# The second hypergraph layer's node table starts as a copy of x, and its rows are scaled before they are added

## The reference

```python
norm_n2e, norm_e2n = De_inv[edge_idx], Dn_inv[node_idx]   # 1/count of the hyperedge, of the node
def _layer(x, ..., W_n2e, W_e2n):
    h = x @ W_n2e
    e = relu(segment_sum(norm_n2e[:, None] * h[node_idx], edge_idx))
    h2 = e @ W_e2n
    return segment_sum(norm_e2n[:, None] * h2[edge_idx], node_idx)
x1 = relu(_layer(x, W0_n2e, W0_e2n))
x2 = _layer(x1, W1_n2e, W1_e2n)
x  = layernorm(x + x2)
```

## Time and profile before

| | |
|---|---|
| median of 3 runs | 6743.85 us (6737.83 to 6748.29) |
| profiled execution, first to last instruction | 6891.4 us |
| POOL busy | 4010.9 us (58%) |
| DVE busy | 4783.1 us (69%) |
| PE busy | 4257.5 us (62%) |
| ACT busy | 3305.7 us (48%) |
| DMA | 1634.06 MB, mean 237 GB/s |
| HBM | read 816.50 MB, written 813.62 MB |

### The profile page before, as it was taken

How to read it: one execution, slowest core, us unless ns; L and a number is a source line. 1 busy time by engine, 2 the same in 40 slices (tenths; PEclk the granted TensorE clock), 3 DMA queues, 4 the chain that set the end, 5 groups by cost and what they waited for, 6 DMA issues and landing times. The chain is left out here.

```text
span 6891.4 us, 79060 instructions
## 1 busy us (share of the span) xinstructions
PE 4257.5 (62%) x18989; PEld 3141.2 (46%) x18989; DVE 4783.1 (69%) x15487; ACT 3305.7 (48%) x7376; POOL 4010.9 (58%) x3167
## 2 busy tenths in 40 slices
PE   2568883038885788499866677988885677600000
PEld 1247773037774666377612223547774566500000
DVE  6635544645454877599599996866665999587666
ACT  0023331013332555288656665758885788633333
POOL 4757776757775788767155426611113666277776
PEclk9779996569998999799978778989998899855555
DMA  7845445864544999799688988989996677477665
GB/s 278 287 121 79 76 75 147 335 197 75 79 76 89 328 350 351 219 326 342 200 293 304 312 273 318 379 290 328 331 336 222 231 258 247 175 261 242 236 227 193
DMA packets 646111, 1634.06 MB, mean 237 GB/s; under 512 B 128454, under 2 KB 283878, under 8 KB 630290
## 3 DMA queue, kind: packets, MB, share of 16 engines
q1 hardware_dynamic: 459954, 1234.83, 51.9%
q0 software_dynamic: 185696, 394.18, 21.4%
HBM read 816.50 MB, written 813.62 MB: 237 GB/s over the span
## 5 line engine op out<-in xcount | busy, mean ns | idle before, releaser
L822 POOL DMA_INDIRECT NS<-e_tot,e_idx x392 | 648.6, 1655 | 298.1 <-ACT e_tot L1080 222.4
L2304 ACT ACTIVATE l_z<-l_a,l_nb,l_rs 128x256 f32<-128x256 f32 x1176 | 612.7, 605 | 411.3 <-DMA out_dram<-l_z,k_ids 248.1
L1691 POOL DMA_INDIRECT l_eg<-HBT,k_nsrc x392 | 461.8, 1178 | 391.2 <-DVEq L1916 151.3
L956 DVE TENSOR_SCALAR e_eq<-e_pk,z_skey 128x128 f32<-128x128 f32 x588 | 204.2, 348 | 637.1 <-DMA NS<-e_tot,e_idx 608.1
L2181 POOL DMA_INDIRECT out_dram<-l_z,k_ids x392 | 432.0, 1102 | 150.9 <-issue 115.1
L1734 PE MATMUL l_pb<-l_jx,k_ones 128*128 128x128 f32 x26 | 4.3, 304 | 788.3 <-DVE l_jx L1971 788.3
L1080 ACT ACTIVATE e_tot<-e_pa 128x520 f32<-128x520 f32 x196 | 118.6, 605 | 759.7 <-DMA NS<-e_tot,e_idx 748.6
L2226 PE MATMUL l_pm<-k_w_L3b,l_zt 128*128 128x258 f32 x1568 | 404.5, 417 | 126.8 <-ACT l_o L2274 121.8
L2475 DVE BATCH_NORM_STATS2 l_bs<-l_a 128x6 f32<-128x256 f32 x1176 | 467.2, 420 | 10.5 <-issue 3.5
L1223 POOL DMA_INDIRECT XH<-n_o,z_home x392 | 398.0, 1015 | 118.1 <-issue 113.1
L2342 ACT ACTIVATE l_a<-l_a,l_eshare 128x64 f32<-128x64 f32 (+1 forms) x1372 | 382.0, 371 | 124.4 <-DVE l_eshare L1953 67.6
(11 more groups left out here) (409 smaller groups left out, 13538.8 us busy)
## 6 DMA issues: line engine op xcount, KB each, us to landing
NS<-z_zero SPq DMA_DIRECT2D x200, 520.0 KB
HBT<-l_o SPq DMA_DIRECT2D x196, 528.0 KB
l_a<-HBT SPq DMA_DIRECT2D x196, 528.0 KB
GSUMS<-l_erun SPq DMA_DIRECT2D x72, 1056.0 KB
l_a<-XH SPq DMA_DIRECT2D x98, 528.0 KB
HA<-n_o SPq DMA_DIRECT2D x98, 528.0 KB
l_a<-HA SPq DMA_DIRECT2D x98, 528.0 KB
n_r<-NS SPq DMA_DIRECT2D x98, 520.0 KB
```

What stands on the lines that cost most here:

```text
L822: pool.indirect_dma_start(out=nodes, out_offset=bass.IndirectOffsetOnAxis(ap=idx[q % DEEP][:, k:k + 1], axis=0), in_=tot[q % 2][:, k, :], ...
L1691: pool.indirect_dma_start(out=self.g[b % self.ng][:, k, :], out_offset=None, in_=self.table, in_offset=bass.IndirectOffsetOnAxis(ap=self.i ...
L2304: last = act.activation(z[:, j, 0:D], a[:, j, 0:D], ACT.Identity, bias=self.nb[b][:, col:col + 1], scale=self.rs[b][:, col:col + 1])
```

## The change

In e1 the clears of NS1 are replaced by copies of x's blocks into NS1, from DRAM to DRAM, at the same place in SP's list: 97 of 512 rows by 256 floats and one of 336 rows. Two small clears of the rows that x does not have (256 dummy rows and 128 rows from N on) come ahead of them. NS1's rows are 256 floats (1024 bytes) and no longer carry a count. The reciprocal counts that DVE makes in the gather half are kept for all 49 tiles (inv is [128, 49, 4]), and ACT's copy of the two sums becomes two activations, one per column, each scaled by that column's inv. PE's sums have 256 columns in e1 in place of 260. The node stage loads NS1 alone (8 slots), its count, reciprocal and add steps go, and statistics are taken from what was loaded. e0 stays as it was: zeros, counts, one copy.

```diff
+def copy_rows(eng, table, x, n, sem):
+    if n == TAILN:
+        eng.dma_start(table[TAIL0:N, :].rearrange("(p j) w -> p (j w)", j=J), x[TAIL0:N, :].rearrange("(p j) w -> p (j w)", j=J)).then_inc(sem, 16)
+    else:
+        eng.dma_start(table[n * BLK:(n + 1) * BLK, :].rearrange("(p j) w -> p (j w)", j=J),
+                      x[n * BLK:(n + 1) * BLK, :].rearrange("(p j) w -> p (j w)", j=J)).then_inc(sem, 16)
+def clear_spare_rows(eng, table, zero, sem):
+    spare = NPAD - 2 * P
+    eng.dma_start(table[spare:NPAD, :].rearrange("(p j) w -> p j w", j=2), zero[:, 0:2, 0:D]).then_inc(sem, 16)
+    eng.dma_start(table[N:N + P, :], zero[:, 0, 0:D]).then_inc(sem, 16)
...
-        inv = [s.sb(f"inv{b}", [P, J]) for b in range(2)]
+        inv = s.sb("inv", [P, TR, J]) if scaled else None
...
-                            pool.wait_ge(clear, 16 * CLEARS)
+                            pool.wait_ge(clear, 16 * filled)
...
-                        pe.matmul(pa[:, 0, 0:SW], e[:, 0, :], mt[:, 0, :], start=True, stop=False)
+                        pe.matmul(pa[:, 0, 0:ow], e[:, 0, :], mt[:, 0, 0:ow], start=True, stop=False)
...
-                        act.activation(tot[q % 2][:], pa[:, :, 0:SW], ACT.Copy).then_inc(s_cp, 1)
+                        if scaled:
+                            for k in range(2):
+                                c = column(q) + k
+                                last = act.activation(tot[q % 2][:, k, :], pa[:, k, 0:ow], ACT.Copy, scale=inv[:, c // J, c % J:c % J + 1])
+                        else:
+                            last = act.activation(tot[q % 2][:], pa[:, :, 0:ow], ACT.Copy)
+                        last.then_inc(s_cp, 1)
...
+                        if x is not None and tick == 0:
+                            clear_spare_rows(sp, nodes_of, S["zero"], sem)
                         for n in range(n0 + (n1 - n0) * tick // TR, n0 + (n1 - n0) * (tick + 1) // TR):
-                            clear_rows(sp, nodes_of, S["zero"], n, sem)
+                            if x is None:
+                                clear_rows(sp, nodes_of, S["zero"], n, sem)
+                            else:
+                                copy_rows(sp, nodes_of, x, n, sem)
...
-    RA, RR, RO = 7, 4, 7
+    RA, RO = 8, 8
...
-                            sp.dma_start(a[t % RA][:], A["x"][t * BLK:(t + 1) * BLK, :].rearrange("(p j) w -> p j w", j=J)).then_inc(s_in[t % RA], 16)
-                        sp.dma_start(r[t % RR][:], T["NS1"][t * BLK:(t + 1) * BLK, :].rearrange("(p j) w -> p j w", j=J)).then_inc(s_rin[t % RR], 16)
+                            sp.dma_start(a[t % RA][:], T["NS1"][t * BLK:(t + 1) * BLK, :].rearrange("(p j) w -> p j w", j=J)).then_inc(s_in[t % RA], 16)
...
-                    count_lk.link(dve.tensor_scalar(iv[:], rt[:, :, D], 1.0, None, ALU.max))
-                    count_lk.link(dve.reciprocal(iv[:], iv[:]))
-                        last = dve.scalar_tensor_tensor(at[:, j, :], rt[:, j, 0:D], iv[:, j:j + 1], at[:, j, :], ALU.mult, ALU.add)
...
-        "NS1": nc.dram_tensor("NS1", (NPAD, SW), F32).ap(),
+        "NS1": nc.dram_tensor("NS1", (NPAD, D), F32).ap(),
...
-                                  up=(T["NS1"], S["cleared1"], 0, CLEARS), homes=(S, V, T), gather=T["HOME"])
+                                  up=(T["NS1"], S["cleared1"], 0, NREAL, A["x"]), homes=(S, V, T), gather=T["HOME"])
```

More of the change, by code:

```diff
@@ L692, in hyper_layer_phase @@
     scaled = tw > D
+    ow = nodes.shape[1]
+    filled = CLEARS if up[4] is None else NREAL + 2
     with Scope(nc, tag) as s:
@@ L711, in hyper_layer_phase @@
         idx = [s.sb(f"idx{b}", [P, 2], I32) for b in range(DEEP)]
-        tot = [s.sb(f"tot{b}", [P, 2, SW]) for b in range(2)]
+        tot = [s.sb(f"tot{b}", [P, 2, ow]) for b in range(2)]
         pt = [s.ps(f"pt{b}", [P, KC, 2, P]) for b in range(2)]
@@ L859, in scale @@
                 def scale(t):
[L860 removed]
+                    gt, iv = g[:, t % RG * J:(t % RG + 1) * J, :], inv[:, t, :]
                     dve.wait_ge(s_g[t % RG], 16 * J * (t // RG + 1))
                     scale_lk.settle(dve)
[L863 removed]
+                    scale_lk.link(dve.tensor_scalar(iv, gt[:, :, D], 1.0, None, ALU.max))
                     yield
                     scale_lk.settle(dve)
[L866 removed]
+                    scale_lk.link(dve.reciprocal(iv, iv))
                     yield
@@ L1142, in first_nodes_phase @@
     TN = NREAL
-    LD, ADD, VAR, NORM, TURN, ZT, PROD, EVICT, STORE = 0, 2, 3, 5, 6, 7, 8, 9, 10
-    RA, RR, RO = 7, 4, 7
+    LD, STAT, VAR, NORM, TURN, ZT, PROD, EVICT, STORE = 0, 2, 3, 5, 6, 7, 8, 9, 10
+    RA, RO = 8, 8
     with Scope(nc, tag) as s:
         a = [s.sb(f"a{b}", [P, J, D]) for b in range(RA)]
-        r = [s.sb(f"r{b}", [P, J, SW]) for b in range(RR)]
         o = [s.sb(f"o{b}", [P, J, XW]) for b in range(RO)]
-        inv = [s.sb(f"inv{b}", [P, J]) for b in range(2)]
         bs = [s.sb(f"bs{b}", [P, 2 * J, 6]) for b in range(2)]
@@ L1306, in variance, with stats @@
                     dve.tensor_scalar(ve[b][:], mv[b][:, :, 1], EPS, None, ALU.add).then_inc(s_var, 1)
-                def add(t):
-                    at, rt, iv = a[t % RA], r[t % RR], inv[t % 2]
-                    dve.wait_ge(s_rin[t % RR], 16 * (t // RR + 1))
-                    count_lk.link(dve.tensor_scalar(iv[:], rt[:, :, D], 1.0, None, ALU.max))
-                    yield
-                    count_lk.settle(dve)
-                    count_lk.link(dve.reciprocal(iv[:], iv[:]))
-                    yield
-                    count_lk.settle(dve)
+                def stats(t):
                     dve.wait_ge(s_in[t % RA], 16 * (t // RA + 1))
                     for j in range(J):
-                        last = dve.scalar_tensor_tensor(at[:, j, :], rt[:, j, 0:D], iv[:, j:j + 1], at[:, j, :], ALU.mult, ALU.add)
-                        if j < J - 1:
-                            yield
-                    last.then_inc(s_u, 1)
-                    yield
-                    dve.wait_ge(s_u, t + 1)
-                    for j in range(J):
-                        stat_lk.link(dve.bn_stats(bs[t // 2 % 2][:, t % 2 * J + j, :], at[:, j, :]))
+                        stat_lk.link(dve.bn_stats(bs[t // 2 % 2][:, t % 2 * J + j, :], a[t % RA][:, j, :]))
                         yield
@@ L1338, in _ @@
                         parts.append(variance(*q))
-                    if tile(tick, ADD) is not None:
-                        parts.append(add(tick - ADD))
+                    if tile(tick, STAT) is not None:
+                        parts.append(stats(tick - STAT))
                     take_turns(parts)
```

15 lines of the change are left out of this document (5 added, 10 removed).

## The result

The changed kernel takes 6705.44 us (median of 4 runs, 6700.97 to 6712.72) beside 6743.44 us for the kernel before (4 runs): 38 us less by the medians. The ratio to runs of the kernel before made beside it is 0.9938 (95% interval 0.9924 to 0.9952), which is 42 us, with 32 to 51 as its interval. The forecast was 6739 in a range of 6712 to 6835. The kernel is faster, where the forecast gave that a chance of 0.34, and the result lies 7 us under the range.

A forecast was written before the change was run, and what follows sets the result against it. It took DMA, closely followed by POOL, to bind the gather stage, POOL's add-landing chain the add stage and POOL the node stage. Terms 12 + 0 - 4 - 4 - 5 - 4 = -5 us gave 6739, range 6712 to 6835.

The forecast's parts named there:

- Step (a): Gather stage of e1: copies of x in place of clears cost more DMA time, +12 us (ends -2, +130).
- a load's price: Gather stage: each copy costs what a DRAM load does, 159 us in all, 25 more than the clears; chance 0.37.
- The rival of the double price: Gather stage: a copy pays for read and write, 258 us in place of 134, total 6825; chance 0.28.
- The rival of the cheap copy: Gather stage: a copy is as cheap as a clear, -2 in place of +12, total 6725; chance 0.25.
- Step (b): Add stage: ACT's two scaled evictions in place of one are hidden, 0 us; +33 if on the chain.
- Step (c): Add stage: POOL's adds of 1024 bytes in place of 1040 save 4 us (ends 0, -28).
- The rival with an early landing: Add stage: shorter rows land earlier so POOL never waits, -28 in place of -4, total 6715; chance 0.10.
- (d): Node stage, steady part: POOL stays the bound and wins only some stretch of its scatters, -4 us (0 to -17).
- (f): Node stage's end: POOL's 3.87 us wait for late slots goes with an eighth slot, -4 us (0 to -5).
- the DMA-bound rival: Node stage: halving the loads frees 51 MB of DMA time, -143 us, total 6601; chance 0.
- if it falls under 5.9, POOL was not the bound: Node stage: scatter spacing forecast at 6.1 us a tile; under 5.9 would refute POOL as the bound.
- Step (e): Node stage's start: one load awaited and less DVE work, less an eighth memset, -5 us (0 to -8).

The follow-up runs named there:

- e1: Not a run: the kernel's second hypergraph layer, where the change is made; its gather stage took 280.9 us before and 279.6 after.
- before_again: The kernel before the change, unchanged, profiled a second time; ratio 0.9994 to the kernel before.
- copy_twice: The changed kernel with every copy of a block of x issued a second time, into a table nothing reads; ratio 1.0130 to the kernel before.
- one_evict: The changed kernel with one unscaled ACT eviction of the two sums in place of two scaled ones, division by count left out; ratio 0.9933 to the kernel before.
- node_dma: The kernel before without the node stage's NS1 loads; DVE's count, reciprocal and adds stay, reading zeros; ratio 1.0002 to the kernel before.
- before8: The kernel before with 8 slots for x's rows and for outputs in the node stage in place of 7; ratio 0.9999.
- junk_two: The changed kernel with four extra DVE scalar_tensor_tensor per node-stage tile, both inputs in SBUF, result unused; ratio 0.9986 to the kernel before.
- junk_one: The changed kernel with four extra DVE bn_stats per node-stage tile, one SBUF input, result unused; ratio 0.9944 to the kernel before.
- node_dve8: The kernel before with both node-stage loads, without DVE's count, reciprocal and adds, and with 8 slots in place of 7; ratio 0.9962.
- root_dve: The changed kernel with the node stage's power -1/2 moved from POOL to DVE as Newton steps; 6648.62 us, ratio 0.9851 to the kernel before.

## Why the prediction was wrong

**Step (a), the copy, wrong.** +12 forecast, -1 measured. Two parts of it failed. "Both nearly bind, DMA more: a transfer made longer here costs something": POOL's own row bound, with 266 us of gathers and issue of some 270 from first to last gather in before_again, and 265 of 269 in after; the earlier trace rows had 270 of 278. What spoke for DMA in the earlier trace rows, 8.5 us of DVE's waits and 23.9 at the end, belongs to the drawn-out execution: the second profile has 0.3 and 10.6, and after 0 and 10.6. The 31 us of idle DMA out of which the +12 was worked are of that execution too: the second profile's share is 0.99 in place of 0.90. In copy_twice, where DMA does bind, its waits show by name (98 us for DVE's run buffers), and the earlier trace rows hold nothing of that size. And a load's price (25 us over the clears) was too dear: the copy costs about 8 us more than the clear, by the estimate above, and these were hidden. The rival of the double price is refuted by copy_twice: it put that copy at 258 us, and it took 128. The rival of the cheap copy comes nearest: stage 304 from 306 forecast, 279.6 from 280.9 measured.

**Step (b), two evictions, right.** 0 forecast; one_evict's interval overlaps after's, and ACT still waits 328 us.

**Step (c), shorter adds, not contradicted.** -4 forecast, -6 measured over the profiles, with an uncertainty as large. The rival with an early landing (-28) is refuted: POOL still waits at each pair. Its 6715 is the number nearest to the result, and it would have been near by luck.

**Steps (d) and (f), the node stage, wrong in size.** -8 forecast, -22 to -26 measured (after's 573.9 us against 595.8 in the forecast's own profile and 600.1 in the second). The reading held: POOL has no room, half the loads are worth nothing (node_dma), the DMA-bound rival is dead, and ACT's 178 us of waiting for slots cost nothing (before8). What failed is the choice of -4 out of "What POOL can win is stretch: 1.019 mean against a median of 0.976 [...] 17 us at most", for want of a cause. The scatters alone won 15 us, nearly that whole bound. The cause is DVE's `scalar_tensor_tensor` (junk_two against junk_one), by all that the runs show through its second SBUF input. The bound also left out the powers, which it lengthens too (the earlier trace rows show 1717 ns, after 1685: 3 us over the stage), and the powers' waits for DVE, 8 us in before_again and 3 in the forecast's profile. Step (f)'s wait of 3.87 us at the end stands in the forecast's profile alone; before_again has none there, so (f) forecast -4 for a wait that the kernel has only at times. The mark "if it falls under 5.9, POOL was not the bound" did not trip: 5.94 a tile in the steady part, from 6.18. Over the whole stage it is 5.87 (6.14 before), since the last tiles carry no powers, so the mark was set too close to tell.

**Step (e), the start, low.** -5 forecast for memset and start together; -10 + 1 measured (30.9 us; the other kernels with after's node stage have 30.8 to 33.3). node_dma (39.9) and node_dve8 (35.3) show that neither part gives it alone: it takes the load and DVE's work.

Terms of -5 should have been -1 + 0 - 6 - 26 - 9 = -42. The range was cut at 6712, and that was too high by the steps' own bounds: (a) at -2, (d) at -17, (e) at -8 and (f) at -5 reach 6712 by themselves, with nothing for (c). Two of these have one cause and so come together.

## What to carry to other kernels

When one engine's row fills a stage, compare the mean of its instructions with their fastest form: the gap is work that another engine takes from it, and whoever issues scatters on POOL should see which DVE instructions with two SBUF inputs run beside them. A long wait shown on an engine that isn't the bound, and a DMA share near 1, are no costs until a run without them says so; here an engine at 0.99 of DMA ran as fast as one at 0.80. Where a stage has two candidates, ask which of them shows waits by name, since the one without any is the bound and transfers beside it are free up to its length.

## What was not expected of the hardware

- A scatter's issue on POOL takes 0.97 to 0.98 us (1.04 right behind a power), and up to 1.26 beside two `scalar_tensor_tensor` of 0.44 us on DVE; `bn_stats`, at the same busy time, leaves it alone.
- Copies from DRAM to DRAM of contiguous 512 KB blocks hardly cost more than stores of zeros from SBUF: a second round of 51.2 MB added 128 us beside gathers and stores, and per 51 MB a copy is some 8 us dearer, an estimate.
- One power of [128, 8] on POOL takes 1.69 us; taking it off POOL won 48 us of the stage.
- PE's granted clock in 2200 to 2600 was 0.93 in after and 1.00 of 2.4 GHz in root_dve, where PE did 1786 matmuls in place of 1611 in the same 400 us. Its cause is open.
